# Two transformer layers with experts on one core: expert output without adding in DRAM, W1 by DMA, handovers in chunks

## The reference, cut to what matters

```python
x = layernorm(x + attention_0(x))          # 8 batches of 256 tokens, 16 heads of 8, rotary
x = layernorm(x + experts_0(x))
x = layernorm(x + attention_1(x))          # keys and values through a latent of 32
x = layernorm(x + experts_1(x))
# experts_0: 8 experts, each takes the 256 tokens with the highest softmax probability
route_vals, routes = top_k(softmax(xf @ Ws + bs).T, 256)
h = gelu(einsum('ekd,edf->ekf', xf[routes], W1) + b1)
out = (einsum('ekf,efd->ekd', h, W2) + b2) * route_vals[..., None]
final = zeros.at[routes].add(out)
# experts_1: 16 experts, each token takes its best 4, weights by a softmax over the 4
logits = -sum((x[:, :, None] - keys)**2, -1) + x @ rw.T + rb
topv, topi = top_k(logits, 4)
fused = sum(softmax(topv)[..., None] * expert_out[topi], axis=2)     # expert_out + b2
```

## Time and profile before

| what | us |
|---|---|
| median of 3 executions | 834.6 |
| lowest, highest | 831.3, 836.78 |
| the profiled execution | 832.95 |
| span of its instructions | 831.1 |
| busy in it: PE, DVE, ACT, POOL | 593.2, 478.9, 486.8, 400.2 |
| mean granted clock of PE | 0.88 of full speed |

### The profile page before, as it was taken

One profiled execution on the slowest core, in us unless ns is written; L12 is line 12 of the kernel. 1 busy time (PEld: TensorE's weight loads), 2 busy tenths in 40 slices (PEclk: granted clock), 3 DMA queues, 4 the chain that ended last, 5 costly groups with the idle time before them and its releaser, 6 DMA issues.

```text
span 831.1 us, 17381 instructions
## 1 busy us (share of the span) xinstructions
PE 593.2 (71%) x4619; PEld 401.6 (48%) x4620; DVE 478.9 (58%) x1801; ACT 486.8 (59%) x1207; POOL 400.2 (48%) x511
## 2 busy tenths in 40 slices
PE   3699999975028654899999996287777777777670
PEld 1244444434017643345444445176666666666660
DVE  4877878824664326658888843854444444444415
ACT  1277777762008733357777775076767667667751
POOL 3955553000017842222223201068888888888860
PEclk9999999995559986569999996589999999999985
...
GB/s 158 126 60 7 237 42 1 1 2 51 0 10 37 45 121 6 216 90 26 108 1 0 2 1 52 7 39 45 40 43 44 40 43 44 40 43 44 40 68 118
DMA packets 68641, 43.63 MB, mean 52 GB/s; under 512 B 15798, under 2 KB 62191, under 8 KB 68594
## 3 DMA queue, kind: packets, MB, share of 16 engines
q1 hardware_dynamic: 51698, 29.73, 12.5%
q0 software_dynamic: 16896, 13.32, 12.0%
...
...
## 4 chain that ended last, share of the span: by engine, by line
PE 32%; DVE 20%; issue 17%; DMA 13%; POOL 13%; ACT 3%; DVEq 1%; POOLq 0%; ACTq 0%; SPq 0%
DMA sum<-rt,idx_s 10%; PE bank L624 7%; POOL prob L574 7%; PE bank L640 5%; PE bank L657 5%; DVE mx L1155 5%; POOL sum L578 3%; POOL hold L571 3%; DVE KB L1196 2%; DMA Y<-sum 2%; PE bank L805 2%; DVE passed L1280 2%; PE bank L774 2%; DMA prob<-xs,idx_g 1%; PE bank L768 1%
## 5 line engine op out<-in xcount | busy, mean ns | idle before, releaser
L1155 DVE TENSOR_REDUCE mx<-bank 128x2 f32<-128x512 f32 x256 | 170.2, 688 | 58.5 <-PE bank L624 55.6
L992 ACT ACTIVATE prob<-bank 128x512 f32<-128x512 f32 x256 | 145.9, 602 | 40.7 <-PE bank L640 37.0
L578 POOL DMA_INDIRECT sum<-rt,idx_s x96 | 152.8, 1592 | 28.7 <-issue 21.4
L1083 ACT ACTIVATE prob<-bank,prob 128x128 f32<-128x128 f32 x384 | 109.8, 370 | 54.3 <-PE bank L886 54.0
L571 POOL TENSOR_TENSOR hold<-ones 128x1 f32<-128x1 f32 x106 | 71.7, 677 | 120.4 <-DVE idx_g L1424 116.5
L624 PE MATMUL bank<-KB,QT 128*128 128x512 f16 x256 | 104.0, 413 | 23.2 <-DVE mx L1155 16.0
L1414 DVE TENSOR_SCALAR_CACHE_REDUCE hit<-bank,slot_at 128x128 f32<-128x128 f32 x96 | 39.9, 416 | 124.3 <-PE bank L895 124.3
L905 PE MATMUL bank<-W,prob 128*128 x768 | 107.9, 284 | 1.5 <-ACT prob L1083 0.9
L886 PE MATMUL bank<-rt,prob 128*128 128x128 f32 x768 | 107.6, 285 | 0.0
L574 POOL DMA_INDIRECT prob<-xs,idx_g x96 | 96.0, 1000 | 16.5 <-issue 14.2
L886 PEld LDWEIGHTS bank<-rt,prob 128*128 128x128 f32 x768 | 97.1, 198 | 1.5
...
## 6 DMA issues: line engine op xcount, KB each, us to landing
...
prob<-xs,idx_g POOLq DMA_INDIRECT x96, 2.6
sum<-rt,idx_s POOLq DMA_INDIRECT x96
...
```

The costliest lines, as they stand in the source:

```text
L578: nc.gpsimd.indirect_dma_start(sums_d[lay][(s - 1) % 2], bass.IndirectOffsetOnAxis(idx_s[:, (s - 1) % 4:(s - 1) % 4 + 1], 0), yo[:, (s - 1 ...
L992: nc.scalar.activation(prob[:, v % 8, :, :], st_bank(i - 1, v)[:, :], ACT.Exp, scale=SCALE).then_inc(exp_done, 1)
L1083: last = nc.scalar.activation(hid[:, s % 2, f, :], bank[2 + s % 2][:, P * f:P * f + P], (ACT.Gelu_apprx_tanh, ACT.Gelu)[lay], bias=wc[:, s ...
L1155: nc.vector.tensor_reduce(m_at, bank[S1B[u % 2]][:, :].rearrange("p (j k) -> p j k", j=2), AX.X, ALU.max).then_inc(s1_used, 1)
```

## The change

Layer 1 no longer adds in DRAM: each token's four outputs go to four slices of a new tensor `parts`, by choice (lowest expert first), with a plain scatter; the row numbers come with the gathered row, behind the gates. POOL computes them (`place_of_each_choice`). Slices 0 to 2 are read while the last experts run, slice 3 in four parts at the end, and DVE and POOL add them. Layer 0 has three sums instead of two; tiles 0 to 3, 14 and 15 are written plainly, the others add. Rows in these tensors are ordered so that a partition's 16 rows are contiguous.

In the slots, `hold` is gone: the gather carries the waits itself, and the scatter follows it. The pipeline is deeper: lists two steps earlier, output three steps after W1 instead of one, steps from -6 to J+3. W1 and its bias come to `wc` by a DMA on SP per tile (layer 1); in layer 0 they are read in place, the expert numbers being known when the program is built, and the output bias is one more product in the bank of L905.

Between attention and experts, 12 of 16 tiles are aggregated, normalised (4 on DVE, 8 on POOL), turned and given logits in the draining iterations; the reciprocal root is a power on POOL. In layer 1 the scores, maxima and comparisons of the 12 tiles are also there. Behind a stage of experts, sums, statistics, norm, turning and output go in four chunks of four tiles, two tiles of a chunk on DVE and two on ACT. In layer 1's attention, batch 0 is projected between the chunks and batch 1 behind the key transposes.

```diff
...
+                e = tile_expert(sp, 1, t, 0, s, sp_experts)
+                if not (isinstance(t, int) and t < 4):
+                    sp.wait_ge(gelu_done, t + NJT[0] - 3)
+                sp.dma_start(wc[:, s, :], W[:, bass.ds(e, 1), 0:W2AT].rearrange("p a f -> p (a f)")).then_inc(wc_in[s], 16)
...
+            def sums_in():
+                for n, qs in ((1, (2, 3)), (0, (0, 1))):
+                    for q in qs:
+                        sp.wait_ge(scattered[q], 48 + 16 * (n == 0))
+                    sp.dma_start(sum_of[n], runs(sums_d[n])).then_inc(sum_back[n], 16)
+                for q in (2, 3):
+                    sp.wait_ge(scattered[q], 64)
                 for c in range(4):
...
+            def choices_in():
+                for k in range(TOPK - 1):
+                    if k == 0:
+                        sp.wait_ge(count_ready, 1)
+                    done = sp.value_load(n_slice[0:1, k:k + 1], min_val=16, max_val=4 * NJT[1])
+                    for q in range(4):
+                        sp.wait_ge(scattered[q], done + 4 * NJT[0])
+                    sp.dma_start(slice_of[k], runs(d["parts"][TOK * k:TOK * k + TOK, :])).then_inc(slice_back[k], 16)
+                for q in range(4):
+                    sp.wait_ge(scattered[q], 4 * (NJT[0] + NJT[1]))
+                for c in range(4):
+                    at = slice(4 * c, 4 * c + 4)
+                    sp.dma_start(slice_of[TOPK - 1][:, at, :],
+                                 runs(d["parts"][TOK * (TOPK - 1):TOK * TOPK, :])[:, at, :]).then_inc(end_back[c], 16)
...
+            def scale(n):
+                t0, t1 = norm_tiles(n)
+                pool.wait_ge(var_ready, n + 1)
+                nc.gpsimd.tensor_scalar(mv[:, t0:t1, 1], mv[:, t0:t1, 1], EPS, None, ALU.add).then_inc(rstd_ready, 1)
+                pool.wait_ge(rstd_ready, n + 1)
+                nc.gpsimd.tensor_tensor(rstd[:, t0:t1], mv[:, t0:t1, 1], mhalf[:, t0:t1], ALU.pow).then_inc(scale_ready, 1)
...
+            def tail_normalise(lay):
+                scale(7 * lay)
+                pool.wait_ge(scale_ready, 7 * lay + 1)
+                for c in (1, 2):
+                    for t in range(4 * c, 4 * c + 4):
+                        last = nc.gpsimd.tensor_scalar(X[:, t, :], Y[:, t, :], mv[:, t, 0:1], rstd[:, t:t + 1],
+                                                       ALU.subtract, ALU.mult)
+                    last.then_inc(tail_pool, 1)
...
-                kd = j + NJT[0] * lay
-                E = (E0, E1)[lay]
-                if not (is_tile(lay, j - 1) or is_tile(lay, j + AHEAD)):
-                    return
-                if is_tile(lay, j + AHEAD):
-                    pool.wait_ge(idx_ready, kd + AHEAD + 1)
-                if is_tile(lay, j - 1):
-                    pool.wait_ge(yo_ready, kd)
-                    pool.wait_ge(idx_s_ready, kd)
-                    wait_for(pool, scattered[(s - 1) % 2], 8 * (kd - 1 - (s - 1) % 2))
-                wait_for(pool, held, (NJT[0] + AHEAD + 1) * lay + j + (AHEAD if isinstance(j, int) else AHEAD - 3))
-                nc.gpsimd.tensor_tensor(hold[:, s:s + 1], ones[:, 0:1], ones[:, 0:1], ALU.mult).then_inc(held, 1)
-                if is_tile(lay, j + AHEAD):
-                    q = (s + AHEAD) % 4
-                    nc.gpsimd.indirect_dma_start(xg[:, q, 0:P + E], None, xs[lay],
-                                                 bass.IndirectOffsetOnAxis(idx_g[:, q:q + 1], 0)
-                                                 ).then_inc(gathered[q], 16)
-                if is_tile(lay, j - 1):
-                    nc.gpsimd.indirect_dma_start(sums_d[lay][(s - 1) % 2],
-                                                 bass.IndirectOffsetOnAxis(idx_s[:, (s - 1) % 4:(s - 1) % 4 + 1], 0),
-                                                 yo[:, (s - 1) % 4, :], None,
-                                                 compute_op=ALU.add).then_inc(scattered[(s - 1) % 2], 16)
+                k = j + NJT[0] * lay
+                if is_tile(lay, j + 4):
+                    pool.wait_ge(idx_ready, k + 5)
+                if is_tile(lay, j - 4):
+                    pool.wait_ge(yo_ready, k - 3)
+                    q, slot, here = (s - 4) % 8, yo[:, s % 4, :], scattered[s % 4]
+                    if lay == 0 and j % 2 == 0:
+                        landed(pool, k - 7, (s - 7) % 4)
+                pool.sem_inc(slot_open)
+                if is_tile(lay, j + 4):
+                    gather(lay, s % 4)
+                if is_tile(lay, j - 4):
+                    to = bass.IndirectOffsetOnAxis(idx_s[:, q:q + 1], 0)
+                    if lay == 1:
+                        nc.gpsimd.indirect_dma_start(d["parts"], to, slot, None).then_inc(here, 16)
+                    elif 4 <= j - 4 < NJT[0] - 2:
+                        nc.gpsimd.indirect_dma_start(sums_d[sum_buffer(j - 4)], to, slot, None,
+                                                     compute_op=ALU.add).then_inc(here, 16)
+                    else:
+                        nc.gpsimd.indirect_dma_start(sums_d[sum_buffer(j - 4)], to, slot, None).then_inc(here, 16)
...
+            def place_of_each_choice():
+                Z = E1 // 2
+                pool.wait_ge(sel_ready, 3)
+                nc.gpsimd.tensor_scalar(cum[0][:, :, Z:Z + E1],
+                                        selz[:, 1:1 + E1 * NT].rearrange("p (e t) -> p t e", t=NT), float(TOK), None,
+                                        ALU.mult).then_inc(rank_step, 1)
+                for n in range(4):
+                    a, sh = n % 2, 1 << n
+                    pool.wait_ge(rank_step, n + 1)
+                    nc.gpsimd.tensor_tensor(cum[1 - a][:, :, Z:Z + E1], cum[a][:, :, Z:Z + E1],
+                                            cum[a][:, :, Z - sh:Z + E1 - sh], ALU.add).then_inc(rank_step, 1)
+                pool.wait_ge(rank_step, 5)
+                nc.gpsimd.tensor_tensor(dest, cum[0][:, :, Z:Z + E1],
+                                        row_base[:, :].unsqueeze(2).to_broadcast([P, NT, E1]),
+                                        ALU.add).then_inc(rank_step, 1)
+            def choices_joined():
+                for c in range(4):
+                    at = slice(4 * c, 4 * c + 4)
+                    pool.wait_ge(part_ready, c + 1)
+                    pool.wait_ge(end_back[c], 16)
+                    nc.gpsimd.tensor_tensor(Y[:, at, :], X[:, at, :], slice_of[TOPK - 1][:, at, :],
+                                            ALU.add).then_inc(last_slice, 1)
+                    if c > 0:
+                        scale_and_shift(join_group(4 + c - 1))
+                scale_and_shift(join_group(7))
             pool.wait_ge(first_in, 16 * N_FIRST)
...
-                                         scale=gcol[:, q:q + 1]).then_inc(yo_ready, 1)
-                if is_tile(lay, j + 2):
-                    e = tile_expert(act, lay, ej_in, j + 4, s, act_experts)
-                    nc.scalar.copy(wc[:, (s + 2) % 4, :], W[:, bass.ds(e, 1), 0:W2AT]).then_inc(wc_ready, 1)
+                if is_tile(lay, j - 3):
+                    q = (s - 3) % 4
+                    act.wait_ge(gcol_ready, k - 2)
+                    landed(act, k - 7, q)
+                    act.wait_ge(eo_done, k - 2)
+                    nc.scalar.activation(yo[:, q, :], bank[6 + q % 2][:, 0:P], ACT.Copy,
+                                         scale=gcol[:, (s - 3) % 8:(s - 3) % 8 + 1]).then_inc(yo_ready, 1)
...
+            def join_chunk(n):
+                at, t0 = slice(4 * (n % 4), 4 * (n % 4) + 4), 4 * (n % 4)
+                for t in range(t0, t0 + 4):
+                    last = nc.vector.bn_stats(stats[:, t, :], Y[:, t, :])
+                step(last)
+                for t in range(t0, t0 + 4):
+                    last = nc.vector.bn_aggr(mv[:, t, :], stats[:, t, :])
+                last.then_inc(var_ready, 1)
+                dve.wait_ge(scale_ready, join_group(n) + 1)
+                for t in range(t0, t0 + 2):
+                    last = nc.vector.tensor_scalar(X[:, t, :], Y[:, t, :], mv[:, t, 0:1], rstd[:, t:t + 1],
+                                                   ALU.subtract, ALU.mult)
+                last.then_inc(join_dve, 1)
...
-                dve.wait_ge(biased, 4 * lay + 4)
+                    at = slice(4 * c, 4 * c + 4)
+                    dve.wait_ge(own_back[c], 16)
+                    step(nc.vector.tensor_tensor(Y[:, at, :], X[:, at, :], own_sum[:, at, :], ALU.add))
+                    join_chunk(c)
+            def choices_summed():
+                dve.wait_ge(xs_in[1], 48)
+                dve.wait_ge(slice_back[0], 16)
+                for k in range(1, TOPK - 1):
+                    dve.wait_ge(slice_back[k], 16)
+                    step(nc.vector.tensor_tensor(Y[:, :, :], Y[:, :, :], slice_of[k], ALU.add))
+                for c in range(4):
+                    at = slice(4 * c, 4 * c + 4)
+                    dve.wait_ge(gb_done, c + 1)
```

(6 more changed lines are left out.)

858 lines of the change are left out of this document (532 added, 326 removed).

## The result

The changed kernel was measured at **855.07 us** (852.39 to 860.93, 4 executions) beside 833.92 for the kernel before: ratio 1.0262, 95% interval 1.0198 to 1.0326. I had forecast 748, with a range of 722 to 788. That is 107 us off and on the wrong side.

The account below looks back on a forecast made before the run. The prediction took POOL's queue in layer 1's slots (3.28 us per step) as the bound. Its terms took the 831.1 us span to 744.4, plus 1.85 around it and 1.65 to the median's level: 748 us, range 722 to 788.

Parts of the forecast that it names:

- Period = 1.00 + 0.30 + 1.05 + 0.30 = 2.65: Layer 1's slots: POOL's gather, gap, plain scatter and gap make a step of 2.65 us, against 3.28.
- C: Slots: W1 loads on the shared DMA engines delay gathers, PE's transpose waits; slower than before, 840 or more; chance 0.04.
- Slots 1: Layer 1's expert slots: 13.6 to first scatter, 71 periods, 14.5 after; 216.5 against 269.2 us, -52.7.
- Join: Layer 0's slots to layer 1's attention, sums in four chunks: 27 against 31.9 us, -4.9.
- The power: POOL's power instead of root and reciprocal: 0.3 us each, bounds 0.19 to 0.85, some ten times on the path.
- Attention 1: Layer 1's attention: DVE's reduction, maxima and scores ahead of two norms add 3.5 us before the last Y.
- the rule that I had called weightless: DVE and GpSimd operations on SBUF can exclude each other: up to 1.5 us at layer 1's rank passes, not counted.
- Attention 0 and slots 0: Layer 0: attention +1.5 us from DVE's work ahead of the last norm; slots 50.0 against 59.6, -9.6.
- layer 1's handover: Layer 1, last Y to first gather, most scores computed earlier: 19.5 against 31.9 us, -12.4.
- rival A: Slots: the plain scatter costs as much as the adding one, 1.59; period 3.15, 784 us; chance 0.20.
- B: Slots: POOL's DMA gaps nearly close or scatters are shorter, PE bounds at 2.3; 723 us; chance 0.17.
- D: Attention-to-slots handovers gain nothing, since DVE's inserted work delays the last batch as much: +25, 773 us; chance 0.09.

Follow-up runs that it names:

- d0: The changed kernel's file unaltered, run again in six executions (also written d0_exact): 776.31 us, ratio 0.9326 to the kernel before.
- g1: The changed kernel with W1 and its bias copied by ACT again in layer 1 and no load on SP's queue: 850.86 us.
- c0_again: The changed kernel's file unaltered, traced a second time: 773.87 us.
- e0: The changed kernel's file unaltered, run once more on another chip: 776.92 us.
- n0: The changed kernel's file unaltered, run in a later session: 773.87 us.
- m1: The changed kernel with POOL's one-column product back in front of gather and scatter in layer 1's slots only: 851.09 us.
- k1: The changed kernel with scatters that add in layer 1 too, into parts filled with zeros on SP's queue: 822.78 us.

## Why the prediction was wrong

**The sign.** It fell with one term, "Period = 1.00 + 0.30 + 1.05 + 0.30 = 2.65". Each summand was right within 0.06, and on record the mean step was 3.66 all the same. What failed is the wait that the sum put at nothing: it takes POOL's own work for the whole step. On record POOL's gather waited for ACT's scaled output 47.7 us between 570 and 770, and ACT and DVE in turn for PE, whose flags came late. In the earlier trace rows nothing hinted at that. The nearest rival was C, but its place (PE waiting for gathers) and its cause (W1 loads) are both refuted: PE's waits for gathers add up to 26.2 us on record and 25.4 in d0, at the upper level the long waits are DVE's and ACT's for PE and POOL's for ACT, and g1 without loads is at 850.9 beside 859.0. My break-even for C was a period of 3.87 with the other gains in place; 3.66 reaches it because those gains were smaller than I had summed.

**The size, at the lower level.** There the forecast is 28 us too low. Term by term, in us of the span (d0_exact beside the prediction):

| stretch | before | predicted | d0 | missed by |
|---|---|---|---|---|
| attention 0 | 186.1 | 187.6 | 191.5 | +3.9 |
| last Y to first gather | 58.6 | 46.2 | 48.1 | +1.9 |
| slots 0 | 59.6 | 50.0 | 54.1 | +4.1 |
| join | 31.9 | 27.0 | 35.6 | +8.6 |
| attention 1 | 170.6 | 174.1 | 177.3 | +3.2 |
| last Y to first gather | 31.9 | 19.5 | 21.6 | +2.1 |
| slots 1 | 269.2 | 216.5 | 220.2 | +3.7 |
| end | 23.2 | 23.5 | 26.3 | +2.8 |

- Slots 1: the total is near, by luck. The first step that scatters came 17.3 us behind the first gather, not 13.6, and the part behind the 71 steps took 19.4, not 14.5; the steps of 2.58 instead of 2.65 gave 4.7 of these 8.6 back.
- Join: wrong in sign. The first add of a chunk (L1686) starts 6.8 us after SP's read, not 3.3, since the 1 MB read of another sum went out 0.4 us ahead of it and its add of 2.29 us stands first. The chunks take 4.0 us each, not 3.3, and the power alone is 0.74 longer than I had taken. Behind the last chunk 12.7 us go by instead of 10.5.
- The power: I took 0.3, bounds 0.19 to 0.85. It takes 0.71 for 2 columns, 1.04 for 4 and 2.30 for 12, so (2.30 - 0.71) / 10 = 0.16 per column. I had bounded it by rows of other operations and picked a value near the lower end with no row behind it.
- Attention 1: no single execution settles this term. The file shows 170.4 at a granted clock of 0.96 (c0_again) and 177.3 at 0.90 (d0, e0, n0), so I am 3.7 too high by the one and 3.2 too low by the other. In all of them, though, the rule that I had called weightless has a place. These two rows of d0_exact overlap:

```profile
494.63 2.75 POOL L689 TENSOR_TENSOR XB<-X 128x1536 f32<-128x1536 f32 x1
494.69 3.02 DVE L1487 TENSOR_SCALAR X<-Y,mv,rstd 128x128 f32<-128x128 f32 x2 [1.18 <-POOL rstd L660]
```

The same pair of DVE operations takes 0.60 at 508.56. Here the first of them lasts 2.77 (0.34 otherwise), until POOL's squares end at 497.38: 2.4 us lost, ahead of the last Y. The other profiles of the file show the same 2.77. The Trainium skill (SBUF — State Buffer, Who interferes with whom) says that GpSimd and a DVE operation that uses the shared port pair shut each other out for a whole instruction. By that rule the wait is as long as what is left of POOL's 2.75, and the trace agrees; that this operation uses the pair is inferred from the wait. I had tried the rule at one place only (the ranks) and dismissed it for all.
- Attention 0 and slots 0: 3.9 and 4.1 over, each without a run of its own. In the slots, the first step that scatters came 15.5 us behind the first gather, not 13.4; the eight steps took 23.6, not 22.4, and the rest 15.1, not 14.2.
- Two sums were off from the start: layer 1's handover lists 3.7 + 6.9 + 5.0 + 3.1 = 18.7 and takes 19.5, and rival A's period is 1.00 + 0.30 + 1.59 + 0.30 = 3.19, not 3.15, which makes it 786 instead of 784.

**The scatter, as predicted.** 1.05 taken, 0.99 measured, and for the reason given: in 600 to 700 us the execution on record has 2198 packets for 55 indirect DMAs, 40 each, against 122 for an adding one (609 for five).

```profile
q0 software_dynamic: 2198, 4.06, 15.1%
```

**Rivals.** A (scatter stays at 1.59) is refuted by the scatter's 0.99 and B (gaps close) by the gaps of 0.30 and the lower level's step of 2.58. D (handovers gain nothing, 773) is the nearest of all to the lower level: outside the long slots I had summed a gain of 34 us, and d0 shows 8. But its mechanism, DVE's work ahead of the last batches, has at most 7 of the missing 26 (the two attentions of d0, which vary with the clock); 9 are in the join, which D didn't name.

**What stays open.** What sets the upper level, and whether PE's matmuls finish late there or only their flags. Shown: it recurs; it hits exactly the stretches of slots; of the engines' flags only PE's are late; it needs neither the loads on SP's queue nor the missing product (each was taken away alone); the transfers themselves are not slower (a W1 packet of 2 KB takes 85 ns at both levels in the trace's packet records); chip 11 had it in one session and not in another, by layer 0's slots, which are the same code in m1 and k1; the kernel before has never had it in 39 executions, on the same chips in the same sessions. Not tried at the upper level: the fast step in the old pipeline, the slow step in the new, and slots without plain scatters; so the plain scatters (S), the pace of the steps and the deeper pipeline all remain possible. At that level the trace also lacks more than half of the flag records of layer 1's slots (2055 against 4740). The Trainium skill (NOTIFIC — the notification-queue block, Overflow: three behaviours, one of which stalls the engine) describes queues of such records that can drop them or hold up who writes them; no run here shows whether late flags and missing records have one cause, and since every execution compared was profiled, none could.
